# Layer 0 attention by four heads and 32 queries at a time, and score matmuls over 64 rows instead of 128

## The chip, the cores and the metric

The kernel runs on one core of one Trainium2 chip. The metric is the device time of one execution in microseconds (us). The engines of a core are TensorE (PE in the profile, with its weight loads as PEld), VectorE (DVE), ScalarE (ACT), GpSimd (POOL) and SyncE (SP), which here issues nearly all the DMAs. TensorE's clock has two levels, 1.2 and 2.4 GHz; the profile gives the granted clock as a share of the higher one.

## The reference

Fourteen sublayers run one after another on an input of 4 batches x 512 tokens x 128 features. Those that matter here are the attentions, all with 16 heads of 8 features:

```
x = x + _L0_attn_ref(_layernorm(x), ...)      # layer 0: a learned bias by distance q - k; keys further back
                                              # than the table of 32 distances get no weight
_L1_ffn_ref:  softmax attention over all earlier keys (causal), then gated experts     # twice
_L1_attn_ref: scores * beta, lower triangle, no softmax
_L2_attn_ref: softmax attention inside blocks of 32 tokens
_L3_attn_ref: softmax attention over all 512 keys
```

Layer 0's scores are `q k^T / sqrt(8) + bias[q - k]`. What the kernel keeps of the bias table is 32 rows (REL = 32), so a query looks at no more than the 31 keys before it and itself.

## The kernel before

**Slots.** The work is cut into 56 units (14 sublayers x 4 batches), and each unit into three parts: pre (normalize, project to q, k and v, bring q and k into the layout for the scores), core (the attention or expert work itself) and post (output projection, residual). The program is a row of 58 slots. In slot k the core of unit k, the pre of unit k+1 and the post of unit k-1 run beside each other, and a barrier of all engines ends the slot. Within a slot each engine has one fixed row of instructions. A table (SLOT_ORDERS, ORDERS) says in which order the three streams take turns on an engine: in "a3b1a1b4" a is the core, b the pre and c the post, and the number says how many steps. An engine waits at a semaphore in that row, and all behind it waits too.

**q and k for the scores.** q and k are split into three bf16 parts each, stacked to 64 columns per head (stack_parts), and turned by TensorE with two heads side by side, so that 128 rows hold two heads (turn_stacks: 8 pairs of heads through one bank of PSUM). k is copied as it stands (KX). q is copied twice per pair by copy_q, the upper half to one slot of QX and the lower half to another, where the other 64 rows are zeros. So score_rows gives 128 rows for q and for k, and the rows of the other head count for nothing. In the two rotary attentions (layers 2 and 3) clear_q writes those zeros first, since QX held other data.

**The scores in attend8** (l1_ffn, l2_attn, l3_attn): a first pass of score matmuls finds each row's maximum (L969, then for the causal kind a 128-row matmul that adds the mask, L972; DVE reduces at L1051); a second pass gives the scores transposed (L1000, mask L1003), ACT takes the exponential (L1094), and TensorE weighs v with it (L1017, 128 rows by 32 columns for each of four heads). Between them the maxima are put into q, which is turned and copied again (take_q, through copy_q, L427).

**Layer 0's core, attend_near.** 64 units: 16 heads x 4 blocks of 128 queries, each against the 256 keys (128 in the first block) up to its end. Per unit: a score matmul (L1139), an add of the bias with the row minimum (DVE L1194), the exponential with its sum (ACT L1173), reciprocal and scaling (DVE L1199, L1202), one or two turns (PE L1148), a copy (ACT L1181), and the weighing of v (PE L1160). The bias comes sheared out of DRAM: the pre writes q times the bias table there (L1257), and the core reads it back with a stride of one less than the row, one DMA per head (L1127), 16 in a core.

Of the kernel before, what the change touches and what calls it, by code (L numbers as in the profile page):

```python
# [30 lines left out]
P = 128  # L31
# [12 lines left out]
REL = 32  # L44
# [14 lines left out]
    [("ip_T", NI), ("pv", 4 * DV), ("l0_qkv", 3 * D), ("l0_out", 4 * D),  # L59
# [8 lines left out]
L0_COLS = NI + 4 * DV + 3 * D + 4 * D  # L68
# [146 lines left out]
def bank(m, i, n=512):  # L215
    return m.ps[:, i, 0:n]
# [198 lines left out]
def q_slot(h):  # L415
    return 4 * (h // 4) + 2 * (h % 2) + (h // 2) % 2


def score_rows(a, h):

    return a.QX[:, q_slot(h), :], a.KX[:, h // 2, :]


def copy_q(copy, a, pair, src):

    for e in range(2):
        ins = copy(a.QX[64 * e:64 * e + 64, q_slot(2 * pair + e), :], src[64 * e:64 * e + 64, :])  # L427
    return ins
# [6 lines left out]
def clear_q(nc, m, lane, a):  # L435

    cleared = lane.note("cleared")

    def gpsimd(pool):
        yield 0.0  # L440
        nc.gpsimd.memset(a.whole[:, 0:4096], 0.0).then_inc(cleared, 1)

    lane.add(0.1, gpsimd=gpsimd)
    return cleared, 1


def turn_stacks(nc, m, lane, a, stkk, ready, cleared=None):
# [15 lines left out]
    def take(eng, copy, pair):  # L463
        if cleared is not None and pair < 2:
            eng.wait_ge(*cleared)
# [444 lines left out]
def attend8(nc, m, note, a, kind):  # L910
# [194 lines left out]
def attend_near(nc, m, note, a, heads, rows_of, value_of, place_of, sheared):  # L1105
    units = [(h, qt) for h in range(heads) for qt in range(NT)]
    U = len(units)
    NS, NPR, NTB, NTS, NAV, NREL = 2, 6, 2, 4, 2, 3
    AVB = NS + NTB
    TURN, WEIGH = 3, 5  # L1110

    def width(qt):
        return 2 * P if qt else P

    scores, negmax, exps, inverted, scaled, turned, pT_ready, av, o_out = (note(n) for n in (
        "scores", "negmax", "exps", "inverted", "scaled", "turned", "pT_ready", "av", "o_out"))
    rel_in = [note(f"rel{i}") for i in range(NREL)]
    prob = m.core[:, 0:NPR * 2 * P].rearrange("p (a b) -> p a b", b=2 * P)
    pT = m.core[:, NPR * 2 * P:(NPR + NTS) * 2 * P].rearrange("p (a b) -> p a b", b=2 * P)
    rel = m.core[:, (NPR + NTS) * 2 * P:(NPR + NTS) * 2 * P + NREL * 2 * L].rearrange("p (h q j) -> p h q j", h=NREL, q=NT)  # L1120

    def sync(sp):
        for h in range(heads):
            yield max(0.0, NT * (h - NREL + 1) + 0.5)
            if h >= NREL:
                sp.wait_ge(negmax, NT * (h - NREL + 1))
            sp.dma_start(rel[:, h % NREL], sheared(h)).then_inc(rel_in[h % NREL], 16)  # L1127

    def tensor(pe):
        for i in range(U + WEIGH):  # L1130
            yield i
            if i < U:
                h, qt = units[i]
                nk = width(qt)
                k0 = (qt + 1) * P - nk
                q, k = rows_of(h)
                if i >= NS:
                    pe.wait_ge(negmax, i - NS + 1)
                nc.tensor.matmul(bank(m, i % NS, nk), q[:, qt * P:(qt + 1) * P], k[:, k0:k0 + nk],  # L1139
                                 start=True, stop=True).then_inc(scores, 1)  # L1140
            if TURN <= i < U + TURN:
                u = i - TURN
                nk = width(units[u][1])
                pe.wait_ge(scaled, u + 1)
                if u >= NTB:
                    pe.wait_ge(pT_ready, u - NTB + 1)
                for c in range(nk // P):
                    ins = nc.tensor.transpose(m.ps[:, NS + u % NTB, c * P:(c + 1) * P],  # L1148
                                              prob[:, u % NPR, c * P:(c + 1) * P], m.weight["ident"])
                ins.then_inc(turned, 1)  # L1150
            if i >= WEIGH:
                u = i - WEIGH
                h, qt = units[u]
                nc_ = width(qt) // P
                at, chunk, last = place_of(h)
                pe.wait_ge(pT_ready, u + 1)
                if at.start == 0 and qt == 0 and chunk >= NAV:
                    pe.wait_ge(o_out, chunk - NAV + 1)
                for c in range(nc_):
                    ins = nc.tensor.matmul(m.ps[at, AVB + chunk % NAV, qt * P:(qt + 1) * P],  # L1160
                                           value_of(h, qt + 1 - nc_ + c), pT[:, u % NTS, c * P:(c + 1) * P],
                                           start=(c == 0), stop=(c == nc_ - 1))
                ins.then_inc(av, 1)

    def scalar(act):
        for i in range(U + TURN):
            yield i + 0.6
            if i < U:
                nk = width(units[i][1])
                act.wait_ge(negmax, i + 1)  # L1170
                if i >= NPR:
                    act.wait_ge(turned, i - NPR + 1)
                nc.scalar.activation(prob[:, i % NPR, 0:nk], prob[:, i % NPR, 0:nk], ACT.Exp, bias=m.nm[:, i:i + 1],  # L1173
                                     scale=-1.0, accum_out=m.sums[:, i:i + 1]).then_inc(exps, 1)
            if i >= TURN:
                u = i - TURN
                nk = width(units[u][1])
                act.wait_ge(turned, u + 1)
                if u >= NTS:
                    act.wait_ge(av, u - NTS + 1)  # L1180
                nc.scalar.copy(pT[:, u % NTS, 0:nk], bank(m, NS + u % NTB, nk)).then_inc(pT_ready, 1)  # L1181

    def vector(dve):
        for i in range(U + WEIGH + 1):
            yield i + 0.3
            if i < U:
                h, qt = units[i]
                nk = width(qt)
                dve.wait_ge(scores, i + 1)
                if qt == 0:  # L1190
                    dve.wait_ge(rel_in[h % NREL], 16 * (h // NREL + 1))
                if i >= NPR:
                    dve.wait_ge(turned, i - NPR + 1)
                nc.vector.tensor_tensor_reduce(prob[:, i % NPR, 0:nk], bank(m, i % NS, nk),  # L1194
                                               rel[:, h % NREL, qt, 2 * P - nk:2 * P], 1.0, -NEG * 4,
                                               ALU.add, ALU.min, m.nm[:, i:i + 1]).then_inc(negmax, 1)
            if 1 <= i <= U:
                dve.wait_ge(exps, i)
                nc.vector.reciprocal(m.rsum[:, i - 1:i], m.sums[:, i - 1:i]).then_inc(inverted, 1)  # L1199
                dve.wait_ge(inverted, i)  # L1200
                p = prob[:, (i - 1) % NPR, 0:width(units[i - 1][1])]
                nc.vector.tensor_scalar(p, p, m.rsum[:, i - 1:i], None, ALU.mult).then_inc(scaled, 1)  # L1202
            if i >= WEIGH:
                u = i - WEIGH
                if u < U:
                    h, qt = units[u]
                    at, chunk, last = place_of(h)
                    if last and qt == NT - 1:
                        dve.wait_ge(av, u + 1)
                        nc.vector.tensor_copy(a.otok[:, chunk, :], bank(m, AVB + chunk % NAV)).then_inc(o_out, 1)  # L1210

    return [(U + WEIGH + 1.0, dict(tensor=tensor, scalar=scalar, vector=vector, sync=sync))]


# [3 lines left out]
def l0_attn_pre(nc, m, lane, a, b, l):  # L1218
# [6 lines left out]
    turn_stacks(nc, m, lane, a, s.stkk, stacked)  # L1225
    f = lane.fills(4)
    stored = lane.note("stored")
    shear = m.shear[a.p]

    def tensor(pe):  # L1230
        for r in range(4):
            yield 3.0 * r
            pe.wait_ge(lane.taken, f + r)
            for i in range(4):
                for qt in range(NT):
                    h = 2 * (4 * (r % 2) + i) + r // 2
# [1506 lines left out]
```

## Time and profile before

| | |
|---|---|
| Runs | 3664.6, 3666.59, 3658.38 us (median 3664.6) |
| The profiled execution | 3654.07 us, its span 3652.2 us |
| Granted TensorE clock, mean | 0.882 |
| PE, PEld, DVE, ACT, POOL busy | 81%, 51%, 66%, 53%, 25% of the span |
| Instructions | 63921, of them 23249 matmuls |
| Layer 0 attention cores | the four slots from 217.8 to 607.1 us |
| Causal cores (l1_ffn, twice) | the eight slots from 775.6 to 1111.6 and from 1375.6 to 1688.6 us |
| Layer 2 and layer 3 attention cores | four slots each, from 1924.0 and from 2794.0 us |

How to read it: the shares are means over slots with different limits. PE's busy time counts the latency of each matmul too, so that its share is not its load; the times from one matmul's start to the next one's tell more. A row of a group of instructions gives its line, engine, operation, output and inputs, for a matmul the tile of the array in use (rows*columns), the shape and the count, then busy time in us and the mean of one in ns, then the idle time before it and what ended it. The page's chain of waits covers only the last slot (its shares are 1% and less), and says nothing of the rest.

### The profile page before, as it was taken

What the parts mean: (1) busy time and instruction counts of PE and PEld (TensorE: products, weight loads), DVE (VectorE), ACT (ScalarE), POOL (GpSimd) and SP (SyncE); (2) the same over time, 40 slices, a digit from 0 to 9 for tenths busy, and PEclk for the clock granted to TensorE, in tenths of its full rate; (3) what the DMA queues carried; (4) which work ended last, traced back from release to release, by engine and by line L of the source; (5) the groups of instructions that cost most, each with busy time, mean ns of one, the idle gap of its engine ahead of it and who ended that gap; (6) DMA issues with size and microseconds to landing.
All of it is one profiled execution on the core that took longest, in us unless ns stands there. A gap on an engine that the chain in (4) does not pass through costs nothing. (4 is left out here: it accounts for less than half of the span.)

```text
span 3652.2 us, 63921 instructions
## 1 busy us (share of the span) xinstructions
PE 2966.9 (81%) x23249; PEld 1869.6 (51%) x23249; DVE 2404.7 (66%) x6402; ACT 1929.6 (53%) x5094; POOL 899.9 (25%) x875
## 2 busy tenths in 40 slices
PE   5868888878987558899787787889887889889875
PEld 3545544544443434456675587656554333556553
DVE  4667765677777456786456543868776677777752
ACT  2356775245553225555246633656664677667652
POOL 1000000011133331111213211635451112444430
PEclk7879988689988779999898988989998899999987
DMA  3423432000000000003660056300000000001010
GB/s 121 166 76 100 110 102 67 1 1 1 1 1 1 1 1 1 1 1 103 222 210 6 12 194 212 100 20 23 14 23 4 1 1 1 21 14 24 13 29 9
DMA packets 132658, 183.41 MB, mean 50 GB/s; under 512 B 48501, under 2 KB 108021, under 8 KB 130682
## 3 DMA queue, kind: packets, MB, share of 16 engines
q1 hardware_dynamic: 129818, 174.14, 15.3%
q8 instruction: 186, 3.05, 0.4%
q0 software_dynamic: 2048, 4.20, 0.3%
q14 instruction: 126, 1.03, 0.1%
q10 hardware_dynamic: 480, 0.98, 0.1%
HBM read 131.90 MB, written 30.61 MB: 44 GB/s over the span
## 5 line engine op out<-in xcount | busy, mean ns | idle before, releaser
L1051 DVE TENSOR_REDUCE nm<-ps 128x1 f32<-128x512 f32 (+4 forms) x832 | 443.3, 564 | 111.8 <-PE ps L972 63.7
L1094 ACT ACTIVATE core<-ps 128x512 f32<-128x512 f32 (+3 forms) x832 | 377.0, 510 | 131.0 <-PE ps L1003 91.7
L274 POOL TENSOR_TENSOR rstd<-ve,weights 128x4 f32<-128x4 f32 x80 | 80.9, 1011 | 1290.4 <-DVE ve L251 1289.9
L969 PE MATMUL ps<-hand 128*128 128x128 bf16 (+3 forms) x1024 | 302.4, 335 | 57.5 <-DVE nm L1051 31.2
L427 ACT COPY hand<-ps 64x512 bf16<-64x512 bf16 x448 | 259.6, 580 | 139.4 <-PE ps L459 100.7
L1000 PE MATMUL ps<-hand 128*128 128x512 bf16 (+3 forms) x1024 | 273.5, 309 | 18.6 <-ACT hand L427 9.4
L1890 POOL TENSOR_TENSOR pre<-pre,sin 128x512 f32<-128x512 f32 x128 | 221.9, 1754 | 241.3 <-ACT pre L1859 225.5
L2006 ACT ACTIVATE core<-ps,nm 128x128 f32<-128x128 f32 x512 | 181.8, 374 | 124.4 <-DVE nm L2021 123.7
L1659 PE MATMUL ps<-hand 128*128 128x128 f32 x1408 | 199.7, 302 | 38.5 <-DMA hand<-in_experts 38.5
L1895 POOL TENSOR_TENSOR ss<-ss,weights 128x16 f32<-128x16 f32 x64 | 194.2, 3035 | 117.4 <-DVE ss L1910 115.9
L1818 PE MATMUL ps<-weights,pre 128*128 128x512 f32 x384 | 207.1, 637 | 17.4 <-ACT pre L1862 17.3
L1659 PEld LDWEIGHTS ps<-hand 128*128 128x128 f32 x1408 | 187.6, 214 | 49.8 <-DMA hand<-in_experts 45.3
L1675 ACT ACTIVATE core<-ps,hand 128x128 f32<-128x128 f32 x352 | 100.7, 370 | 202.6 <-PE ps L1659 202.3
L969 PEld LDWEIGHTS ps<-hand 128*128 128x128 bf16 x1024 | 99.9, 104 | 198.1 <-DVE nm L1051 135.2
L459 PE MATMUL ps<-identb,hand 128*128 128x128 bf16 x768 | 83.8, 238 | 142.2 <-DVE pre L387 65.7
L1017 PE MATMUL ps<-core,hand 128*32 128x512 f32 (+3 forms) x2048 | 185.0, 451 | 8.7 <-ACT core L1094 5.3
L1000 PEld LDWEIGHTS ps<-hand 128*128 128x128 bf16 x1024 | 94.8, 99 | 185.3 <-ACT core L1094 102.8
L1689 DVE SCALAR_TENSOR_TENSOR core<-ps,hand,core 128x128 f32<-128x128 f32 x352 | 99.0, 344 | 133.2 <-ACT core L1675 132.0
L1173 ACT ACTIVATE core<-core,nm 128x256 f32<-128x256 f32 (+1 forms) x256 | 123.7, 483 | 107.8 <-DVE nm L1194 105.1
L1061 POOL CAST hand<-nm 128x16 bf16<-128x16 f32 x192 | 61.4, 320 | 463.9 <-DVE nm L1051 455.6
L427 DVE COPY hand<-ps 64x512 bf16<-64x512 bf16 x192 | 80.8, 421 | 137.4 <-PE ps L459 135.8
L1160 PE MATMUL ps<-core,hand 128*32 128x128 f32 x896 | 154.4, 294 | 0.0
(331 smaller groups left out, 7542.6 us busy)
## 6 DMA issues: line engine op xcount, KB each, us to landing
hand<-in_experts SPq DMA_DIRECT2D x88, 836.0 KB, 4.9
core<-shear SPq DMA_DIRECT2D x64, 512.0 KB, 3.8
shear<-post SPq DMA_DIRECT2D x64, 256.0 KB
hand<-hand SPq DMA_DIRECT2D x16, 512.0 KB, 4.4
hand<-hand SPq DMA_DIRECT2D x16, 384.0 KB, 5.6
pre<-sorted_in SPq DMA_DIRECT2D x8, 704.0 KB, 4.7
sorted_out<-core SPq DMA_DIRECT2D x88, 64.0 KB, 2.3
core<-in_stream SPq DMA_DIRECT2D x2, 2048.0 KB, 7.8
```

Of the source, the lines that this page charges most:

```text
L427: ins = copy(a.QX[64 * e:64 * e + 64, q_slot(2 * pair + e), :], src[64 * e:64 * e + 64, :])
L969: ins = nc.tensor.matmul(b[:, n * P:n * P + nk], q[:, qt * P:(qt + 1) * P], k[:, lo:lo + nk], start=kind != BLOCK32, stop=True, skip_group ...
L1000: ins = nc.tensor.matmul(b[:, n * P:n * P + z - s], k[:, kt * P:(kt + 1) * P], q[:, s:z], start=kind != BLOCK32, stop=True, skip_group_che ...
L1017: ins = nc.tensor.matmul(m.ps[32 * j:32 * j + 32, OUT, s:z], a.V[:, kt, 9 * h:9 * h + 32], prob8[:, (4 * f + j) % PROBS, n * P:n * P + z - s],
L1051: nc.vector.tensor_reduce(nm_of(h, qts), src, AX.X, ALU.max, negate=True).then_inc(negmax, 1)
L1094: nc.scalar.activation(prob8[:, i % PROBS, 0:L - q0], m.ps[:, RING[at % NR], 0:L - q0], ACT.Exp).then_inc(ring_out, 1)
L1160: ins = nc.tensor.matmul(m.ps[at, AVB + chunk % NAV, qt * P:(qt + 1) * P], value_of(h, qt + 1 - nc_ + c), pT[:, u % NTS, c * P:(c + 1) * P ...
L1659: ins = nc.tensor.matmul(m.ps[:, 2 * (i % 2) + s, c * P:(c + 1) * P], w1(i, s, c), a.xs[:, i * P:(i + 1) * P], start=True, stop=True)
L1818: nc.tensor.matmul(banks[at % N], s.hT[:, t * P:(t + 1) * P], qkv[:, l, i, :], start=True, stop=True).then_inc(lane.filled, 1)
L1890: ins = nc.gpsimd.tensor_tensor(o[:, :, :, z:z + hl], x[:, :, :, y0:y0 + hl], sn[:, t, :, z:z + hl].unsqueeze(2).to_broadcast([P, 2, LH, h ...
L1895: nc.gpsimd.tensor_tensor(m.ss[:, 1, 0:2 * LH], m.ss[:, 0, 0:2 * LH], m.weight["half"][:, 0:2 * LH], ALU.pow).then_inc(rooted, 1)
L2006: nc.scalar.activation(prob[:, i % NP3, r * P:(r + 1) * P], bank(m, S[i % 2])[:, r * P:(r + 1) * P], ACT.Exp, bias=m.nm[:, 4 * i + r:4 * i ...
```

## The change

1. Layer 0's core is written anew (attend_near goes, the code stands in l0_attn_core). 8 units: 4 groups of four heads x 2 halves of 256 queries. A unit's bank holds 8 blocks of 32 queries x 64 keys for four heads, the heads on 32 partitions each. 32 score matmuls of 64 rows by 32 columns make it, DVE adds the bias, takes minima and subtracts them (three instructions over 512 columns), ACT takes one exponential, four turns, one copy, and 32 small matmuls weigh v. The bias is read by 64 DMAs of 32 KB (16 per group), and each of the 32 descriptors x 4 is 256 bytes long.
2. The sums come from v's column of ones, so the post divides and then projects (divide, out_project), where it only projected before.
3. A second copy of v, shifted by 32 tokens (Vs), is made by two DMAs in the pre, after turn_stacks.
4. q is kept once: turned q and k of a pair are one copy of 1024 columns (QK), score_rows gives 64 rows, and copy_q, q_slot and clear_q go. All score matmuls of l1_ffn, l1_attn, l2_attn and l3_attn then use 64 rows; their masks are still 128-row matmuls.
5. The tables of orders are new for the slots with attentions.

```
@@ score_rows, turn_stacks
-    return a.QX[:, q_slot(h), :], a.KX[:, h // 2, :]
+    rows = slice(64 * (h % 2), 64 * (h % 2) + 64)
+    return a.QX[rows, h // 2, :], a.KX[rows, h // 2, :]
...
-        copy_q(copy, a, pair, lane.atb[:, 0:L])
-        copy(a.KX[:, pair, :], lane.atb[:, L:2 * L]).then_inc(lane.taken, 1)
+        copy(a.QK[:, pair, :], lane.atb).then_inc(lane.taken, 1)
@@ attend8, take_q
-            copy_q(nc.scalar.copy, a, 2 * g + n, m.psb[:, RING[at % NR], 0:L]).then_inc(ring_out, 1)
+            nc.scalar.copy(a.QX[:, 2 * g + n, :], m.psb[:, RING[at % NR], 0:L]).then_inc(ring_out, 1)
@@ l0_attn_pre
+    def vector(dve):
+        yield 0.0
+        dve.wait_ge(*stacks_turned)
+        nc.vector.memset(a.Vs[0:32, 0, :], 0.0).then_inc(none_set, 1)
     def sync(sp):
+        yield 0.1
+        sp.wait_ge(*stacks_turned)
+        sp.dma_start(a.Vs[32:128, :, :], a.V[0:96, :, :]).then_inc(moved, 16)
+        sp.dma_start(a.Vs[0:32, 1:NT, :], a.V[96:128, 0:NT - 1, :]).then_inc(moved, 16)
@@ l0_attn_core
+    units = [(g, half) for g in range(4) for half in range(2)]
+    BQ, BK = 32, 64
+    NPR, NTS, NREL = 3, 3, 2
+    def sync(sp):
+        for g in range(4):
+            yield max(0.0, 2.0 * (g - NREL + 1) + 0.6)
+            if g >= NREL:
+                sp.wait_ge(added, 2 * (g - NREL + 1))
+            for j in range(4):
+                for odd in range(2):
+                    for r in range(2):
...
+                        sp.dma_start(dst[:, :, odd, r], src).then_inc(rel_in[g % NREL], 16)
+        def score(i):
+            if half == 0:
+                nc.tensor.matmul(out[:, 0:BK], m.identb, m.far, start=True, stop=True)
+            for n, at, _, _ in blocks(half):
+                for j in range(4):
+                    q, k = score_rows(a, 4 * g + j)
...
+                    ins = nc.tensor.matmul(out[BQ * j:BQ * (j + 1), at:at + BK], q[:, BQ * n:BQ * (n + 1)], keys, ...)
+        def weigh(u):
+            for n, at, v, row in blocks(half):
+                for j in range(4):
+                    ins = nc.tensor.matmul(m.ps[BQ * j:BQ * (j + 1), O[row // BK], to:to + BQ],
+                                           v[row:row + BK, 9 * h:9 * h + 32], pT[row:row + BK, u % NTS, col:col + BQ], ...)
+    def vector(dve):
+            if half == 0:
+                dve.wait_ge(rel_in[g % NREL], 16 * 16 * (g // NREL + 1))
+            nc.vector.tensor_tensor(p, bank(m, S[i % 2]), rel[:, g % NREL, half * L:(half + 1) * L], ALU.add)
+            nc.vector.tensor_reduce(lows(i), eight(p), AX.X, ALU.min)
+            nc.vector.tensor_tensor(eight(p), eight(p), lows(i).unsqueeze(2).to_broadcast([P, 8, BK]), ALU.subtract)
@@ l0_attn_post
-    project_turned(nc, m, lane, a.otok, m.weight["l0_out"], m.x[b])
+    divided = divide(nc, m, lane, a.otok, m.post.ot)
+    out_project(nc, m, lane, m.post.ot, m.post.oT, m.weight["l0_out"], None, m.x[b], m.x[b], divided)
@@ the order of slots 5 and 6 (a core, b pre, c post)
-     "sync": "a15b1a1b4"},
+     "sync": "a3b1a1b5"},
```

On SP in a slot that holds layer 0's core of batch 1 and its pre of batch 2 (slot 5; slot 6 is the same). "core" is the bias buffer, "hand" the buffers that pre hands to core, "shear" the sheared bias in DRAM. Before:

```order
45 L1127 DMA core<-shear 128x4x256 x15
46 L1257 DMA shear<-pre 128x16x32
47 L1127 DMA core<-shear 128x4x256
48 L1257 DMA shear<-pre 128x16x32 x3
```

And of the change:

```order
46 L1183 DMA core<-shear 32x4x64 x48
47 L1122 DMA hand<-hand 96x672
48 L1123 DMA hand<-hand 32x504
49 L1183 DMA core<-shear 32x4x64 x16
50 L1132 DMA shear<-pre 128x16x32 x4
```

The fourth group's 16 bias loads stand behind the two moves of v, which wait for the end of turn_stacks.

On DVE in slot 6 of the change, from its start. L1246, L1249 and L1252 are the add, minimum and subtract of a unit; L371 begins stack_parts of the pre:

```order
436 L1246 TENSOR_TENSOR core<-ps,core 128x512
437 L1249 TENSOR_REDUCE nm<-core 128x8
...
443 L1246 TENSOR_TENSOR core<-ps,core 128x512
444 L1249 TENSOR_REDUCE nm<-core 128x8
...
448 L1246 TENSOR_TENSOR core<-ps,core 128x512
449 L1249 TENSOR_REDUCE nm<-core 128x8
450 L371 CAST hand<-pre 128x64x8
```

Two whole units, and the add and the minimum of the third (the first that needs the second group's bias), stand ahead of the pre's stacking.

On ACT in slot 7 (layer 0's core of batch 3 beside l0_ffn's pre, whose GELU is L727), of the change; L1260 is the core's exponential, L1267 and L1274 its copies:

```order
230 L727 ACT_TABLE_LOAD
231 L727 ACTIVATE pre,acc_pre<-ps 128x512
232 L1260 ACT_TABLE_LOAD
233 L1260 ACTIVATE core<-core 128x512
234 L1267 COPY core<-ps 128x512
235 L727 ACT_TABLE_LOAD
```

There are 14 loads of a table in this slot of the change, and 16 before.

## Rows read from the trace of the kernel before

**Rows 1.** Windows, last two layer 0 slots and sum: stretch, length, busy, PEclk, DMA share, GB/s.

```profile
406.50:493.90 87.40, 74.09 (x572) 46.65 (x572) 66.83 (x296) 61.45 (x224) 5.07 (x9) 0.94 0.41 109
493.90:607.10 113.20, 89.39 (x532) 51.48 (x532) 64.99 (x298) 77.21 (x227) 1.01 (x1) 0.83 0.26 75
sum 389.30, PE 318.69 PEld 195.06 DVE 272.76 ACT 264.52 POOL 16.28; mean PE 79.67 PEld 48.77 DVE 68.19 ACT 66.13 POOL 4.07
```

**Rows 2.** Groups of instructions in slot 6, 406.5 to 493.8 us.

```profile
L1173 ACT ACTIVATE core<-core,nm 128x128 f32<-128x128 f32 (+1 forms) x64 | 31.0, 484 | 24.2 <-DVE nm L1194 23.5
L1194 DVE CUSTOM_DVE_ANT_0 core<-ps,core 128x128 f32<-128x128 f32 (+1 forms) x64 | 24.8, 388 | 9.0 <-PE ps L1139 8.3
```

**Rows 3.** SP's timeline: start us, length us, then engine, line, operation, count.

```profile
84.11 21.42 SPq L2475 DMA_DIRECT2D shear<-post  x32
```

**Rows 4.** The bias loads of line 1127 by themselves, over the whole run.

```profile
L1127 SPq DMA_DIRECT2D core<-shear x64: 359/360/2142, 217.9 to 577.7; - x64
...
DMA to landing us min/median/max: 3.5/3.8/6.2
```

**Rows 5.** Groups by form, VectorE, whole run.

```profile
L2029 DVE TENSOR_TENSOR core<-core,rsum 128x512 f32<-128x512 f32 x128 | 97.1, 759 | 4.4
L2021 DVE TENSOR_REDUCE nm<-ps 128x4 f32<-128x512 f32 x128 | 87.8, 686 | 78.7 <-PE ps L1973 70.6 <-DMA post<-y 7.4
...
L468 DVE COPY hand<-ps 128x512 bf16<-128x512 bf16 x96 | 40.8, 425 | 1.3
```

**Rows 6.** Groups by form, ScalarE, whole run.

```profile
L427 ACT COPY hand<-ps 64x512 bf16<-64x512 bf16 x448 | 259.6, 580 | 139.4 <-PE ps L459 100.7 <-PE ps L983 32.6
...
L468 ACT COPY hand<-ps 128x512 bf16<-128x512 bf16 x96 | 56.3, 586 | 1.1
```

**Rows 7.** VectorE's timeline at the end of slot 17 (l1_attn), slot 18 begins in the last row.

```profile
1250.10 0.86 DVE L427 COPY hand<-ps 64x512 bf16<-64x512 bf16 x2 [4.02 <-PE ps L459]
...
1255.42 0.85 DVE L427 COPY hand<-ps 64x512 bf16<-64x512 bf16 x2 [4.02 <-PE ps L459]
...
1259.51 0.68 DVE L242 BATCH_NORM_STATS2 st<-x 128x6 f32<-128x128 f32 x3 [2.79 <-PEq L206]
```

**Rows 8.** ScalarE's table loads in slot 7.

```profile
L752 ACT ACT_TABLE_LOAD x8 | 10.3, 1283 | 0.1
L1173 ACT ACT_TABLE_LOAD x8 | 10.3, 1283 | 0.1
```

**Rows 9.** The first of the three instructions of a rank comparison, whole run.

```profile
L691 DVE TENSOR_SCALAR pre<-pre,acc_pre 128x128 bf16<-128x128 f32 (+3 forms) x64 | 33.0, 515 | 37.9 <-ACT pre L755 28.2 <-PE ps L704 9.3
```

**Rows 10.** Windows: one causal slot (slot 13), and the sum of all eight.

```profile
849.60:934.70 85.10, 77.37 (x584) 39.31 (x584) 66.45 (x188) 48.22 (x116) 14.12 (x31) 0.90 0.00 1
...
sum 649.00, PE 577.36 PEld 301.83 DVE 488.21 ACT 382.56 POOL 125.65; mean PE 72.17 PEld 37.73 DVE 61.03 ACT 47.82 POOL 15.71
```

**Rows 11.** TensorE's timeline in slot 13, matmuls alone.

```profile
871.25 0.23 PE L212 MATMUL ps<-rowparts,onesb 3*128 3x128 bf16 x1
871.41 0.39 PE L1000 MATMUL ps<-hand 128*128 128x512 bf16 x1
871.63 0.22 PE L1003 MATMUL ps<-identb,negcausal 128*128 128x128 bf16 x1
871.69 0.22 PE L969 MATMUL ps<-hand 128*128 128x128 bf16 x1
```

**Rows 12.** TensorE's timeline in slot 37 (layer 3's local attention).

```profile
2414.52 0.38 PE L1967 MATMUL ps<-negwin,identb 128*128 128x512 bf16 x1
2414.83 1.09 PE L1973 MATMUL ps<-hand 64*64 64x128 f32 x16
```

**Rows 13.** TensorE's timeline in slot 3.

```profile
208.85 0.17 PE L704 MATMUL ps<-onesb,post 128*128 128x1 bf16 x1
208.95 0.37 PE L814 MATMUL ps<-aggv,hand 64*128 64x1 f32 x1
```

**Rows 14.** Waits in slot 13: waiter, waited for, us in total, times, longest.

```profile
PEld ps L969 <- DVE nm L1051: 8.3, 18, 1.1
```

More of the change, by code:

```diff
@@ L412, in stack_parts, with turn_stacks @@
     return stacked, 3
-def q_slot(h):
-    return 4 * (h // 4) + 2 * (h % 2) + (h // 2) % 2
 def score_rows(a, h):
-    return a.QX[:, q_slot(h), :], a.KX[:, h // 2, :]
[L424 to L428, printed above, removed]
+    rows = slice(64 * (h % 2), 64 * (h % 2) + 64)
+    return a.QX[rows, h // 2, :], a.KX[rows, h // 2, :]
 def pair_of(stk, t, pair):
     return stk[:, t, 2 * pair:2 * pair + 2, :].rearrange("p a b -> p (a b)")
[L435 to L447, printed above, removed]
+def turn_stacks(nc, m, lane, a, stkk, ready):
     f = lane.fills(8)
@@ L1102, in attend8 @@
     return [(LEAD + total + 1.0, dict(tensor=tensor, vector=vector, gpsimd=gpsimd, scalar=scalar))]
[L1105 to L1212, printed above, removed]
@@ new lines, in l0_attn_core @@
+    U = len(units)
+    BQ, BK = 32, 64
+    NPR, NTS, NREL = 3, 3, 2
+    TURN, WEIGH = 2, 3
+    S, PT, O = (0, 1), (2, 3), (4, 5)
+    scores, added, least, shifted, exps, turned, pT_ready, av, o_out = (note(n) for n in (
+        "scores", "added", "least", "shifted", "exps", "turned", "pT_ready", "av", "o_out"))
+    rel_in = [note(f"rel{i}") for i in range(NREL)]
+    prob = m.core[:, 0:NPR * L].rearrange("p (s n) -> p s n", s=NPR)
+    pT = m.core[:, NPR * L:(NPR + NTS) * L].rearrange("p (s n) -> p s n", s=NTS)
@@ new lines, in scalar @@
+    def scalar(act):
+        for i in range(U + WEIGH + 1):
+            if i < U:
+                yield i + 1.4
+                act.wait_ge(shifted, i + 1)
+                nc.scalar.activation(prob[:, i % NPR, :], prob[:, i % NPR, :], ACT.Exp, scale=-1.0).then_inc(exps, 1)
+            if TURN <= i < U + TURN:
+                yield i + 1.6
+                u = i - TURN
+                act.wait_ge(turned, u + 1)
+                if u >= NTS:
+                    act.wait_ge(av, u - NTS + 1)
+                nc.scalar.copy(pT[:, u % NTS, :], bank(m, PT[u % 2])).then_inc(pT_ready, 1)
+            if i >= WEIGH and (i - WEIGH) < U and units[i - WEIGH][1] == 1:
+                yield i + 1.8
+                g = units[i - WEIGH][0]
+                act.wait_ge(av, i - WEIGH + 1)
+                own = a.otok[:, g, :].rearrange("p (t r n) -> p r t n", r=2, n=BK)
+                out = m.ps[:, O[0]:O[1] + 1, 0:L // 2].rearrange("p r (t n) -> p r t n", n=BK)
+                nc.scalar.copy(own, out).then_inc(o_out, 1)
@@ L2312, in macaron @@
             a.whole = whole
-            a.QX, a.KX = (whole[:, s:z].bitcast(BF16).rearrange("p (h n) -> p h n", n=L) for s, z in ((0, 4096), (4096, 6144)))
+            a.QK = whole[:, 0:4096].bitcast(BF16).rearrange("p (c n) -> p c n", c=8)
+            a.QX, a.KX = a.QK[:, :, 0:L], a.QK[:, :, L:2 * L]
             v = 6144
@@ L2400, in macaron @@
         m.EX = sb("EX", REL, dt=BF16)
+        m.far = sb("far", 64, dt=BF16)
         totals = [offsets(fields)[1] for fields in LEVELS]
```

279 lines of the change are left out of this document (172 added, 107 removed).

## Prediction

> **What bounds the kernel now.** The page's shares are means over 58 slots, and its chain of waits shows only the last slot, so I read the windows first, one per slot, then the groups inside a slot, and last the starts of single matmuls. Layer 0's four core slots take 389.3 us together, slot 6 87.4 and slot 7 113.2 [rows 1]. There no engine is full, but three are near it: of the 1.37 us that slot 6 has per unit (64 of them) PE is busy in 1.16, DVE in 1.04 and ACT in 0.96, and they hand the same tile round. ACT alone has 64 exponentials of 0.48 and stands 23.5 us before them, waiting for DVE's 64 adds [rows 2]. Slot 7 adds 16 table loads of 1.28 us [rows 8]. The eight causal slots take 649 us, PE busy in 577 of them [rows 10]. In these PE is packed: a mask starts 0.22 us after a 512-column score matmul and the next score 0.06 us after the mask [rows 11], which is one column per 0.42 ns with nothing between. So TensorE's own time is the bound in the second pass. Ahead of it, some 22 score matmuls wait for DVE's maxima, 8.3 us in all [rows 14].
>
> **Layer 0, slots 4 to 7.** The 64 units go, and with them nearly all of what rows 1 show as busy beside the pre. What comes is 8 units. On DVE each costs three instructions over 512 columns: 0.69 + 0.69 + 0.76 = 2.1 us [rows 5] (the add taken like the reduction), 17 us in all. On ACT 8 x 0.6 + 12 copies x 0.6 = 12 us [rows 6] (a copy of as many columns). On PE 64 small matmuls and 4 turns per unit. No row has a tile of 64*32; 16 matmuls on tiles of 64*64 take 1.09 us with 128 columns [rows 12], 0.07 each, so 64 lie between 64 x 0.025 and 64 x 0.07 = 1.6 to 4.5 us, and I take 2.5. The core by itself would then need 8 x 2.5 + 6 = 26 us.
>
> It won't get that, since SP must issue 64 bias loads where there were 16. The issue itself is 0.36 us long [rows 4]; 32 loads of 128 descriptors in a row took 21.42 us, 0.67 each [rows 3]. The new ones have 128 descriptors as well, so I take 0.65 and keep 0.36 as the other end. From issue to landing it is 3.8 us [rows 4]. A group of 16 then lands every 10.4 us: 14, 25, 35 and 45 us after the slot's start.
>
> - Slots 5 and 6: DVE's row has the add and minimum of the third unit ahead of the pre's stacking, so stacking starts at 26 rather than near 18. It takes 6 us. turn_stacks has 8 pairs. Now two pairs take 5.32 us [rows 7]. The copies of a pair shrink from 2 x 0.58 + 0.59 to about 1.0 on ACT and from 2 x 0.42 + 0.42 to about 0.8 on DVE (one copy of 1024 columns, from the fixed part and the slope between 0.58 for 64x512 and the time of 512 columns; an estimate from [rows 5, 6]), 0.6 us per pair and 4.9 per pre. That gives 8 x 1.9 = 15, and the stacks are turned at 47. Behind that on SP stand the two moves of v (1.3) and the last 16 loads (10.4), landed at 62.5. Two units on DVE (4.4) and the tail through exponential, turns, copy, weighing and the copy out (3.8), and the barrier (1): 71. At 0.36 per issue it is 58.
> - Slot 7: the last group lands at 45, DVE has all core steps ahead of the eight rank comparisons of the next l0_ffn. 45 + 4.4 + 8 x 1.3 (the first of three instructions is 0.5 [rows 9]) + 1.5 = 62; 14 table loads stay (18 us on ACT), which are hidden beside these loads. At 0.36: 50.
> - Slot 4: SP has all four groups ahead of the pre's stores, and the post of l0_ffn adds 10 us of DVE: 62, or 52.
>
> Sum 71 + 71 + 62 + 62 = 266, less about 4 for an issue between the two ends: 262 against 389, **-127 us**; the ends are 218 and 285. The longer post (16 turns, four reciprocals and products, one projection, about 8 us in a row) lies beside slots of over 60 us, in slot 8 beside the core of l0_ffn; I give it nothing, 2 us if it shows.
>
> **The causal slots.** The instructions are the same in number and columns, but 128 score matmuls per slot now use a tile of 64*128 with a 128*128 mask behind each. A change of tile has a price in this trace. K = 3 rows to 128: 0.16 us from start to start where 128 columns alone take 0.06 [rows 11], so 0.10. 128*128 to 64*64: 0.31 after 512 columns where 0.22 is due, so 0.09 [rows 12]. 128*128 to 64*128, the very pair: 0.10 after one column [rows 13]; before it such matmuls start every 0.025, so 0.07. I take 0.093. Along the order a slot has 79 changes before and 307 after, 228 more, 21 us. In the first 22 scores (44 changes, 4 us) PE waits for DVE anyway [rows 14]; of the rest some 3 us fall into other waits. That leaves 14 us per slot, for eight slots **+112 us**. The ends: 8 us each if the waits swallow twice as much (+64), 20 each if none (+160).
>
> The Trainium skill, TensorEngine Tiling (Array Packing), Key Properties, says that a change of tiling mode drains TensorE. It gives no figure; by that rule both ways cost, as I have counted.
>
> **Other slots.** Layer 3's full attention has no mask, so only 40 changes more per slot (+3.7), but successive heads now lie in different rows. In rows 12, 16 matmuls of 0.107 us of columns take 1.09 instead of 1.7 us: two tiles run at once. At 42 such neighbours of 0.2 us a slot could save 8. With four ACT us less in take_q I put -4 per slot, **-16** (from -30 to +12, if they don't overlap).
>
> The Trainium skill, TensorE: Matmul & The Clock Gate, Part 3, says that matmuls in different row groups run side by side. By that rule the whole 8 us per slot come where PE is the bound, by the rows on 64*64 tiles alone nothing is certain for 64*128.
>
> Layer 2: 62 changes more (5.8) against 4.9 less in turn_stacks and the 3.5 us clearing of q gone: 0. l1_attn: in slots 17 and 18 turn_stacks ends the slot [rows 7], -5 each; elsewhere it ends it with another stream beside it, -1 to -2 in five slots; 15 more changes in four slots hide behind GpSimd's powers. Together **-16** (-30 to +5).
>
> **Sum.** 3652.2 - 127 + 112 - 16 - 16 = 3605 us of span, 1.9 more for the execution. The profiled execution was 10.5 us under the median of the runs; the same step of -47 from 3664.6 gives **3617 us**.
>
> **Rivals.**
> A. The drains cost more than layer 0 saves. Place: the second pass of the causal slots. With +20 per slot, layer 3's overlap absent (+12), and layer 0 held at 285 by SP: 3664.6 + 160 + 12 - 104 - 10 = 3722. It decides from 13 us per causal slot at that layer 0, and from 20 at the layer 0 of my forecast. For it: PE is packed there [rows 11]. Against: the first pass waits for DVE.
> B. The drains hide. If a 64*128 and a 128*128 matmul follow each other without a gap, the causal slots gain 2 us each by the shorter copies, layer 3's slots 3.7 more than forecast, and all is 3664.6 - 127 - 16 - 31 - 16 = 3475. Against it are rows 11 to 13, all three with a gap.
> C. SP issues as fast as its instruction is long, 0.36 us: layer 0 falls to 218, and the time is 3573. For it: 0.36 in rows 4; against: rows 3.
> D. The change doesn't shorten layer 0 since the small tiles issue slowly: at 0.1 us per matmul a unit needs 6.4 us of PE, a core 51 us more or less as SP's loads allow; it would add 10 us per slot, 3657, no change. Little speaks for it.
>
> **Numbers.** Forecast as it stands 0.48, C or between 0.19, B 0.08, A 0.15, D 0.10. About 0.2%, 7 us, is what can be told from no change. Faster: forecast, C and B with a part of D, 0.79; within 0.2% 0.07; slower 0.14 (A, and the upper edge of the others). The likeliest's own range is 3575 to 3660. B and the far end of A are left out: 3540 to 3690.
>
> **What would show it.** Slots 4 to 7 near 62, 71, 71 and 62 us, SP's bias loads 0.65 apart, DVE's adds of units 0, 2, 4 and 6 waiting for the landing, in slots 5 and 6 the last of them after the moves of v. In the causal slots about 98 us instead of 85, and from a score's start to its mask's start 0.09 more than the columns. Layer 3's slots a few us shorter, with scores of two heads starting within 0.01 us. Wrong it is if causal slots stay at 85 (B), or if layer 0's last groups land before 30 us (C).

## The result and the profile after

The changed kernel takes 3902 us (median of four, 3881 to 3920) where the kernel before takes 3662: ratio 1.065, 95% interval 1.060 to 1.071. Forecast were 3617 us and a range of 3540 to 3690. It is slower by 240 us, on the side of rival A but far beyond it. The two profiled executions, from which the times of slots come, are 227 us apart.

The windows, cut at the slots, give first the last two core slots of layer 0 with the sum of all four (columns as in [rows 1]), then two causal slots with the sum of all eight, to be held against [rows 10].

```profile
342.03:409.13 67.10, 39.01 (x972) 29.25 (x972) 31.10 (x61) 22.31 (x45) 6.58 (x9) 0.63 0.34 54
409.13:464.97 55.84, 40.11 (x932) 27.13 (x932) 30.07 (x70) 36.90 (x54) 1.01 (x1) 0.68 0.26 40
sum 252.49, PE 158.71 PEld 115.72 DVE 130.07 ACT 105.68 POOL 20.76; mean PE 39.68 PEld 28.93 DVE 32.52 ACT 26.42 POOL 5.19
```

```profile
748.68:878.54 129.86, 127.41 (x584) 51.93 (x584) 66.54 (x180) 43.06 (x100) 12.91 (x31) 0.63 0.00 1
...
1769.51:1911.64 142.13, 140.00 (x543) 55.78 (x543) 61.99 (x183) 36.94 (x84) 12.20 (x27) 0.52 0.03 8
sum 1028.56, PE 1008.07 PEld 410.97 DVE 491.83 ACT 344.58 POOL 118.45; mean PE 126.01 PEld 51.37 DVE 61.48 ACT 43.07 POOL 14.81
```

Layer 0 gave back 137 us (389 to 252). The causal slots took 380 (649 to 1029). PE has as many instructions there as before (584 in slot 13), is busy 98% of the time, and its granted clock is 0.52 to 0.65 where it was 0.89 to 0.96. Everything else together is about -15: slot 3 -6, l1_attn -13, l3_attn -5, l2_attn +4.5, the rest +4.6.

The first causal slot of the changed kernel in five windows shows how the clock goes.

```profile
632.30:638.00 5.70, 4.59 (x16) 1.59 (x16) 5.09 (x19) 0.00 (x0) 3.23 (x6) 0.66 0.01 4
638.00:643.00 5.00, 4.71 (x20) 2.82 (x20) 4.40 (x13) 1.17 (x2) 0.00 (x0) 0.50 0.00 0
643.00:650.00 7.00, 7.00 (x24) 3.10 (x23) 3.03 (x7) 1.51 (x5) 1.25 (x5) 0.50 0.01 2
650.00:735.00 85.00, 84.87 (x424) 32.66 (x423) 36.33 (x80) 33.08 (x77) 6.49 (x18) 0.53 0.00 1
735.00:748.70 13.70, 12.20 (x130) 6.98 (x126) 3.25 (x6) 8.28 (x19) 0.00 (x0) 1.00 0.00 1
```

The clock falls to 0.50 (1.2 GHz) in the first scores and stays near it for 85 us of attention. The profile calls PE wholly busy there. It is back at 1.00 (2.4 GHz) only in the last 14 us, in which turns and other products over all 128 rows (24 of turn_stacks, 16 of the post) stand among the last scores. Whether these bring it back isn't shown.

The fall at the head of a causal slot is not new. The kernel before has it too, here in slot 13 (from 849.6), and the clock is back after 10 us:

```profile
850.00:860.00 10.00, 8.14 (x37) 2.80 (x36) 9.13 (x30) 0.00 (x0) 1.25 (x3) 0.55 0.01 2
860.00:870.00 10.00, 8.79 (x67) 6.36 (x66) 7.68 (x22) 4.71 (x9) 3.12 (x8) 0.94 0.00 0
```

By the clock's own record in the two traces, no stretch at the lower level lasts longer than 10.2 us in the eight causal slots of before. In the changed kernel each of the eight has one of 61 to 137 us. So what the change did is to keep the clock from coming back, more than to make it fall.

TensorE's timeline shows a pair of units in slot 13, first at the higher level, then at the lower (start us, length us).

```profile
771.10 0.39 PE L975 MATMUL ps<-hand 64*128 64x512 bf16 x1
771.41 0.23 PE L978 MATMUL ps<-identb,negcausal 128*128 128x128 bf16 x1
771.58 0.39 PE L944 MATMUL ps<-hand 64*128 64x512 bf16 x1
771.89 0.23 PE L947 MATMUL ps<-negcausal,identb 128*128 128x128 bf16 x1
...
787.58 0.29 PE L978 MATMUL ps<-identb,negcausal 128*128 128x128 bf16 x1
787.80 0.61 PE L944 MATMUL ps<-hand 64*128 64x512 bf16 x1
788.34 0.29 PE L947 MATMUL ps<-negcausal,identb 128*128 128x128 bf16 x1
788.57 0.39 PE L975 MATMUL ps<-hand 64*128 64x256 bf16 x1
```

At the higher level a mask starts 0.32 us after its 512-column score, 0.22 in [rows 11]: 0.10 for the change, as forecast, and 0.10 more for the way back. At the lower level it is 0.54, of which 0.43 are columns: the change costs 0.11 there, hardly more, and the columns cost double.

With that each start-to-start time can be split. For the eight causal slots I count the columns at the granted clock (twice for f32, and once where two products run side by side), the changes of tile shape at 0.105 us each (the table has their number), and what is left of the slots' time as waiting. So each row adds up: 649 = 445 + 552 x 0.105 + 146.

| kernel | causal slots, us | clock in them | columns, us | changes | waiting, us |
|---|---|---|---|---|---|
| before | 649 | 0.89 to 0.96 | 445 | 552 | 146 |
| after | 1029 | 0.52 to 0.65 | 697 | 2400 | 80 |
| e1: 128 rows | 649 | 0.90 to 0.96 | 444 | 552 | 147 |
| e12: 128 rows, no masks | 633 | 0.85 to 0.93 | 403 | 552 | 172 |
| e11: 64 rows, no masks | 686 | 0.66 to 0.87 | 437 | 883 | 156 |
| e2: 64 rows, masks of 64 rows | 726 | 0.65 to 0.91 | 499 | 883 | 134 |
| e3: 128 rows, masks of 64 rows | 934 | 0.74 to 0.89 | 587 | 2472 | 87 |
| e10: 64 rows, masks together | 872 | 0.59 to 0.89 | 603 | 1728 | 88 |

From before to after: 1848 changes more at 0.105 are +194 us, waiting -66, the same columns at a lower clock +252. That is the 380. Only e2 and e11 have products side by side in these slots (neighbours on opposite halves of the rows that start within 0.03 us): 557 and 211 pairs, which hide 44 and 47 us of columns. Their columns at the granted clock would be 543 and 484 without it.

### The profile page after: what moved, and what is told of

Its sections match the earlier page's. It is cut to its first block and busy times, and to the rows that moved or that the text cites. A ratio compares the mean times of both kernels' runs of the same rounds, so it can differ in the third digit from the quotient of the medians.

```text
span 3879.1 us, 64317 instructions
## 1 busy us (share of the span) xinstructions
PE 3279.5 (85%) x24849; PEld 1889.7 (49%) x24849; DVE 2237.5 (58%) x5304; ACT 1653.9 (43%) x4088; POOL 865.9 (22%) x867
## 5 line engine op out<-in xcount | busy, mean ns | idle before, releaser
L1026 DVE TENSOR_REDUCE nm<-ps 128x1 f32<-128x512 f32 (+4 forms) x832 | 457.3, 564 | 436.4 <-PE ps L947 364.1
L1069 ACT ACTIVATE core<-ps 128x512 f32<-128x512 f32 (+3 forms) x832 | 397.8, 505 | 475.4 <-PE ps L978 409.3
L944 PE MATMUL ps<-hand 64*128 64x128 bf16 (+3 forms) x1024 | 344.6, 389 | 45.7 <-DVE nm L1026 25.6
L975 PE MATMUL ps<-hand 64*128 64x512 bf16 (+3 forms) x1024 | 304.1, 357 | 3.2 <-ACT core L1069 2.5
L992 PE MATMUL ps<-core,hand 128*32 128x512 f32 (+3 forms) x2048 | 230.4, 546 | 5.6 <-ACT core L1069 3.8
L975 PEld LDWEIGHTS ps<-hand 64*128 64x128 bf16 x1024 | 83.4, 97 | 257.2 <-issue 127.5
L944 PEld LDWEIGHTS ps<-hand 64*128 64x128 bf16 x1024 | 90.3, 101 | 192.5 <-DVE nm L1026 93.4
L443 ACT COPY hand<-ps 128x1024 bf16<-128x1024 bf16 x96 | 97.5, 1016 | 139.8 <-PE ps L437 139.5
L443 DVE COPY hand<-ps 128x1024 bf16<-128x1024 bf16 x96 | 66.3, 691 | 143.2 <-PE ps L437 143.0
L1978 PE MATMUL ps<-hand 64*64 64x128 f32 (+1 forms) x2048 | 146.8, 288 | 0.0
L947 PE MATMUL ps<-negcausal,identb 128*128 128x128 bf16 x512 | 143.4, 280 | 0.0
```

Of the source, the lines that this page charges most:

```text
L443: copy(a.QK[:, pair, :], lane.atb).then_inc(lane.taken, 1)
L944: ins = nc.tensor.matmul(b[:, n * P:n * P + nk], q[:, qt * P:(qt + 1) * P], k[:, lo:lo + nk], start=kind != BLOCK32, stop=True, skip_group ...
L975: ins = nc.tensor.matmul(b[:, n * P:n * P + z - s], k[:, kt * P:(kt + 1) * P], q[:, s:z], start=kind != BLOCK32, stop=True, skip_group_che ...
L992: ins = nc.tensor.matmul(m.ps[32 * j:32 * j + 32, OUT, s:z], a.V[:, kt, 9 * h:9 * h + 32], prob8[:, (4 * f + j) % PROBS, n * P:n * P + z - s],
L1026: nc.vector.tensor_reduce(nm_of(h, qts), src, AX.X, ALU.max, negate=True).then_inc(negmax, 1)
L1069: nc.scalar.activation(prob8[:, i % PROBS, 0:L - q0], m.ps[:, RING[at % NR], 0:L - q0], ACT.Exp).then_inc(ring_out, 1)
```

## The experiments

Times of slots are from each kernel's profiled execution, whole times are medians (of two runs for e2, e3, e8, e10, e11 and e12, of four or five for the others), and each ratio is to the kernel before timed beside it (3653 to 3669 us). The edits are shown shortened.

**e1_l0_part.** The layer 0 half alone:

```diff
-            q, k = score_rows(a, h)
+            q, k = all_rows(a, h)   # a.QX[:, q_slot(h), :], a.KX[:, h // 2, :], as before
```

> The layer 0 half of the change alone: the new core, its Vs moves, its divide post; q is kept in zero-filled slots again and every attention but layer 0's reads 128 rows. If the two halves only add, the slots 4 to 7 come to the 252 us of the changed kernel (389 before) and the eight causal slots to the 649 us of before, at a granted clock of 0.89 to 0.96: 3662 - 137 = about 3525 us. If the loss of the causal slots came in part from layer 0 or from the rest of the change, these slots stay over 700 us and the kernel over 3580.

3529 us, ratio 0.965 (0.962 to 0.969). The causal slots are those of before to 0.1 us:

```profile
725.27:810.39 85.12, 77.42 (x584) 39.32 (x584) 66.41 (x188) 48.18 (x116) 14.12 (x31) 0.90 0.00 1
...
sum 648.88, PE 576.02 PEld 301.34 DVE 488.08 ACT 382.30 POOL 125.64; mean PE 72.00 PEld 37.67 DVE 61.01 ACT 47.79 POOL 15.71
```

So layer 0's half costs the causal slots nothing. Layer 0's slots are 267, not 252: the shorter copies of the q half are worth 14 us there.

**e8_q_once.** The other half alone, on the layer 0 of before (with attend_near, whose scores then come by way of the 64-row score_rows).

```diff
-    return a.QX[:, q_slot(h), :], a.KX[:, h // 2, :]
+    rows = slice(64 * (h % 2), 64 * (h % 2) + 64)
+    return a.QX[rows, h // 2, :], a.KX[rows, h // 2, :]
```

> The q half of the change alone, on the layer 0 of before. If the halves add: 3902 + 3653 - 3529 = about 4026 us, with the eight causal slots near the 1029 us of the changed kernel. Layer 0's core then scores over 64 rows too and changes tile shape 3 times a unit instead of twice, so up to 4080 if that costs clock in slots 4 to 7 as it does in the causal slots. Under 3980 would mean that the new layer 0 itself worsened what follows.

4099 us, ratio 1.118 (1.113 to 1.123), beside a before of 3669. The causal slots take 1056 and layer 0's 442, 53 more than before. That is beyond the sum of the halves: the old layer 0 core scores over 64 rows there too, and the causal slots are 27 us longer than in the changed kernel with the same code, 20 of them in slot 14 (149 us for 130, at a clock of 0.50 for 0.63). What made that slot slower isn't shown. The loss is all in this half.

**e2_masks64.** No change of shape inside a unit:

```diff
-                ins = nc.tensor.matmul(b[:, nk - P:nk], m.identb, m.negcausal, start=False, stop=True, ...)
+                rows = slice(64 * (h % 2), 64 * (h % 2) + 64)
+                for other in (0, 1):   # second copies of both with their halves swapped
+                    ins = nc.tensor.matmul(b[:, nk - P:nk], m.eyes[rows, other, :], m.causals[rows, other, :], ...)
```

> The changed kernel, with each causal mask product of 128 rows replaced by two of 64 rows on the head's own half, so that a score and its mask have one tile shape. It has one 128-column product more per score, and no tile-shape change inside a unit. Theory W (the waits at tile-shape changes pull the granted clock down): the clock in the causal slots comes back to 0.88 or more and their sum from 1029 to about 650 us, the kernel to about 3520. Theory R (products over 64 rows, half of the array's rows, do not hold the clock, with or without the waits): the clock stays at 0.50 to 0.68, only the waits themselves go (about 256 of 0.105 us a slot, less some 7 us for the added products), the sum falls to about 890 us and the kernel to about 3765.

3584 us, ratio 0.980 (0.976 to 0.984).

```profile
788.84:878.07 89.23, 82.56 (x712) 44.74 (x712) 66.15 (x180) 40.84 (x100) 14.03 (x31) 0.89 0.01 1
...
1492.15:1598.77 106.62, 101.40 (x671) 52.91 (x671) 60.07 (x183) 34.51 (x84) 12.21 (x27) 0.65 0.04 10
sum 726.15, PE 668.94 PEld 364.40 DVE 482.15 ACT 325.88 POOL 124.01; mean PE 83.62 PEld 45.55 DVE 60.27 ACT 40.74 POOL 15.50
```

With 128 products more in a full slot it is 302 us shorter in the causal slots: 1517 changes fewer are 159, the columns are 198 less (44 of them hidden side by side), and 54 come back as waiting. Most of the clock is back (0.89 in slot 14), not all (0.65 in slot 23). Theory R, that 64 rows alone hold the clock down, falls in its strong form. W, that only the waits do (650 us were expected by it), is not whole either.

**e3_drains128.** e1 with the same masks: 128-row scores, as many changes as in the changed kernel.

> e1_l0_part with the masks alone as two products of 64 rows: the scores fill 128 rows, and there are as many tile-shape changes as in the changed kernel. Theory W: the granted clock in the causal slots falls to about 0.6, their sum is near 1030 us and the kernel near 3900. Theory R: the clock stays at 0.85 or more, a slot gains 256 changes of 0.105 us less what idle hides, and some 5 us of added products: 25 to 30 us a slot, a sum of 850 to 890 us and the kernel near 3740.

3822 us, ratio 1.046 (1.040 to 1.051).

```profile
753.75:870.95 117.20, 113.90 (x712) 49.38 (x712) 68.10 (x188) 50.58 (x116) 14.11 (x31) 0.84 0.00 1
...
1601.27:1727.39 126.12, 122.95 (x712) 52.39 (x712) 68.27 (x188) 50.66 (x116) 14.10 (x31) 0.76 0.00 1
...
sum 934.00, PE 906.71 PEld 399.60 DVE 503.28 ACT 402.17 POOL 123.93; mean PE 113.34 PEld 49.95 DVE 62.91 ACT 50.27 POOL 15.49
```

285 us over e1: 1920 changes 202, 1024 added products of 0.055 us 56, waiting -60, and 87 from the clock, which falls to 0.74 to 0.89. That lies between the two theories (1030 and 850 to 890 us; the sum is 934). About as many changes went with 252 us of clock where the scores fill 64 rows too. The masks of e3 fill 64 rows as well, so this isn't changes alone.

**e11_64_no_mask, e12_128_no_mask.** The cleanest pair: the causal masks are left out of the changed kernel and of e1.

```diff
-            if kind == CAUSAL:
-                ins = nc.tensor.matmul(b[:, nk - P:nk], m.identb, m.negcausal, ...)
```

> The changed kernel with the causal mask products left out (its causal attentions then see all keys up to the block's end): 64-row scores with no tile-shape change between them and no product added. If 64-row products alone do not hold the clock, it stays at 0.75 or below in the causal slots and their sum above 750 us. If only the waits at the changes pulled it down, it is 0.9 as in e12_128_no_mask and the sum 600 to 640, the kernel about 3470 to 3500. If both count, each in part, the clock is 0.80 to 0.88 and the sum 640 to 700.

> e1_l0_part with the causal mask products left out too: 128-row scores, the partner of e11_64_no_mask. A mask product takes 0.055 us of TensorE, 128 of them 7 us a slot; part of that turns into waiting for DVE, so the causal slots fall from 649 to 600 to 625 us at a clock of 0.92 or more, and the kernel from 3529 to about 3490. If the masks' columns were what held the clock up, it falls below 0.88.

3541 and 3518 us (ratios 0.969, 0.966 to 0.972, and 0.963, 0.960 to 0.966). Slot 13 and the sum, first of e11, then of e12:

```profile
708.42:801.39 92.97, 86.38 (x456) 35.24 (x456) 64.34 (x180) 40.44 (x100) 13.87 (x31) 0.69 0.00 1
...
sum 685.67, PE 610.81 PEld 257.36 DVE 473.53 ACT 321.81 POOL 123.65; mean PE 76.35 PEld 32.17 DVE 59.19 ACT 40.23 POOL 15.46
```

```profile
722.22:800.88 78.66, 68.96 (x456) 31.45 (x456) 65.83 (x188) 47.99 (x116) 14.13 (x31) 0.93 0.00 1
...
sum 632.77, PE 543.89 PEld 247.96 DVE 485.11 ACT 380.29 POOL 125.48; mean PE 67.99 PEld 31.00 DVE 60.64 ACT 47.54 POOL 15.69
```

With the same products and columns, and no mask, 64 rows cost 53 us. By the split above that is 35 for 331 changes (those to the turns and the weighing), 34 for the columns, and 16 less waiting. The 34 is what remains of a larger loss: without the 47 us that run side by side in e11, the lower clock costs some 80. So with few changes 64 rows go with a lower clock too. The sum is what was expected if both count in part (640 to 700), the clock is lower than that (0.66 to 0.87 for 0.80 to 0.88). e11 even has a lower clock than e2, which has more products in each unit. My 600 to 625 for e12 was too low: of 56 us of masks left out only 16 came off, 25 turned into waiting, and the clock fell a little.

**e10_masks_together.** Fewer changes, nothing else:

```diff
-            shifted_score(i)      # score, mask
-            score(LEAD + i)       # score, mask
+            side_by_side(shifted_score(i), score(LEAD + i))   # score, score, mask, mask
```

> The changed kernel with another order inside a step of the causal attention: both scores over 64 rows first, then both masks over 128, so that 42 of the 64 steps change tile shape 2 times instead of 4: 84 of some 300 changes of a slot fewer. If a change only costs its own 0.093 to 0.105 us, the causal slots come from 1029 to about 960 us and the kernel to about 3830. If the waits at the changes also hold the clock down, their clock rises from 0.59 to 0.70 or more, and the sum falls below 900, the kernel below 3780.

3714 us, ratio 1.017 (1.014 to 1.019); the causal slots 872. Of the 157 us less, 672 changes are 71 by themselves and the clock is 94, while 8 come back as waiting. A good quarter of the changes gone gives back over a third of what the clock had cost.

**e4_l1_l3_64.** e1 with 64-row scores in l1_attn and l3_attn, and the long copies of q.

```diff
-                    q, k = all_rows(a, 4 * g + j)
+                    q, k = score_rows(a, 4 * g + j)   # a.QX[rows, q_slot(h), :]; likewise where kind is FULL
```

> e1_l0_part, but the scores of l1_attn and of l3_attn read 64 rows (q still in its zero-filled slots, so the copies are those of before). If the 13 us that slots 16 to 19 and the 5 us that slots 44 to 47 gained in the changed kernel come from scores of two heads running side by side, they are here again: 18 us below e1_l0_part, about 3507. If they come from the shorter copies of q instead, it equals e1_l0_part. If the 64 rows cost clock there too, l3_attn's clock is under 0.90 and the kernel no faster than e1_l0_part.

3553 us, ratio 0.972 (0.969 to 0.975), so slower than e1. l1_attn is 264.5 as in e1 (264.1). l3_attn's four slots are 366 where e1 has 346, at a clock of 0.81 to 0.88. The changed kernel's -13 and -5 thus came from shorter copies, and reading 64 rows cost layer 3 some 20 us, though 127 of its score neighbours start side by side.

**e5_pairs64.** e2, with the heads of a step on opposite halves:

```diff
-        return 4 * g + j, second[u]
+        return 4 * g + (j ^ SWAP), second[u]   # SWAP is 1 in the causal and the full attention
-            shifted_score(i)
-            score(LEAD + i)
+            side_by_side(shifted_score(i), score(LEAD + i))
```

> e2_masks64 (3584 us), with the shifted score and the score of one step taken from heads on opposite halves of the rows and issued one after the other (score, score, mask halves alternating), in the causal and in the full attention, so that the two run side by side. If overlap is worth what its columns are, the causal slots lose some 36,000 columns each at 2.4 GHz, part of it into stalls: about 5 us a slot, and layer 3's four slots about 5 each: 3584 - 60 = about 3525 us. If the granted clock goes by how many rows work at a time, the clock in the causal slots also comes up from the 0.65 to 0.91 of e2_masks64 to above 0.88 everywhere, and the time is 3480 to 3500. If instead more overlap means fewer busy cycles and a lower clock, the clock falls below that of e2_masks64 and the time is 3584 or more.

3535 us, ratio 0.964 (0.961 to 0.967). The causal slots are 684 (e2 726), layer 3's 333 (e2 344), with the clock at 0.76 to 0.93. In the causal slots that is the 40 us expected: 743 pairs start side by side where e2 has 557, the columns are 42 us less, and changes and waiting are the same. A part of the 42 is a slightly higher clock. In layer 3 it is half of the 20 expected. The overlap doesn't make 64 rows better than 128 in the causal slots (649).

**e6_two_layouts, e7_loads_first, e9_full_pairs.** Short copies and 64 rows in layer 0, l1_attn and l3_attn; zero-filled q and 128 rows in the causal and block attention, cleared by GpSimd before. e7 moves one thing in two slots, e9 adds the heads of e5 in the full attention:

```diff
-     "sync": "a3b1a1b5"},
+     "sync": "a4b6"},
...
+    SWAP = int(kind == FULL)
-        return 4 * g + j, second[u]
+        return 4 * g + (j ^ SWAP), second[u]
```

> The new layer 0; q kept once and read over 64 rows in layer 0, l1_attn and l3_attn; zero-filled q, 128 rows, cleared by GpSimd ahead of each use (3.5 us), in the causal and block attentions. From e1_l0_part (3529): slots 3 to 7 get the shorter copies of the changed kernel (-20 us), slots 16 to 19 its -13, slots 44 to 47 its -5: about 3491 us, if the clears lie beside other work. If a clear at the head of GpSimd's queue delays the norm of the same pre, slots 11 and 19 are 3 to 4 us longer: about 3498. If the losses of 64-row reads that e4_l1_l3_64 showed in layer 3 (+20) count here too, about 3511.

> e6_two_layouts with one thing moved: in slots 5 and 6 SyncE issues the 16 bias loads of the last group ahead of the two Vs moves (which wait 17 us for the stacks), not behind. If these loads are what ends the slots, as the prediction had it, each of the two is 7 to 10 us shorter: 14 to 20 us below e6_two_layouts. If the copies or TensorE end them, within 3 us of it.

> e7_loads_first, with the shifted score's head taken from the other half of the rows in the full attention alone, so that it runs beside the score that is issued next to it. In e5_pairs64 the four slots of layer 3 came to 333.5 us so, against 344 to 348 in e6 and e7: 10 to 14 us below e7_loads_first (3500), about 3488. If the gain there was luck of the clock, the slots stay near 345 and the time at 3500.

3508, 3500 and 3490 us; ratios 0.958 (0.955 to 0.960), 0.955 (0.952 to 0.958) and 0.956 (0.954 to 0.958). All three beat both kernels. Their times don't tell them apart; single slots do. e6 is 17 us above its forecast by the median (beside a before of 3669, where the forecast built on 3653), 4 by its profiled span (3495); slots 3 to 7 are 20 us shorter than in e1 and l1_attn 11, as expected, and layer 3 only 1. SyncE's timeline in slot 6, of the changed kernel and of e7:

```profile
342.09 25.19 SPq L1183 DMA_DIRECT2D core<-shear  x48
383.92 0.53 SPq L1122 DMA_DIRECT2D hand<-hand  x1
384.49 0.60 SPq L1123 DMA_DIRECT2D hand<-hand  x1
385.43 10.90 SPq L1183 DMA_DIRECT2D core<-shear  x16
396.38 5.20 SPq L1132 DMA_DIRECT2D shear<-pre  x4
```

```profile
335.09 38.25 SPq L1219 DMA_DIRECT2D core<-shear  x64
376.10 0.53 SPq L1158 DMA_DIRECT2D hand<-hand  x1
```

The queue stood 17 us for the stacks with 16 loads behind it. With these ahead, slots 5 and 6 take 60.6 and 60.9 us instead of 68.3 and 66.4 (7 to 10 us each were expected). In e9 the layer 3 slots are 338 (e7 348), and TensorE's timeline has the two scores of a step side by side, twice:

```profile
2859.70 0.39 PE L1009 MATMUL ps<-hand 64*128 64x512 bf16 x1
2859.71 0.39 PE L978 MATMUL ps<-hand 64*128 64x512 bf16 x1
...
2860.58 0.39 PE L1009 MATMUL ps<-hand 64*128 64x512 bf16 x1
2860.58 0.39 PE L978 MATMUL ps<-hand 64*128 64x512 bf16 x1
```

That this is worth 10 us is less sure than it looks. Seven kernels have the layer 3 code of e7, and their four slots range from 341 to 348 us, with e7 the slowest. Against them e9 (338) and e5 (333) are 3 to 14 us shorter.

## Why the prediction was wrong

**The failed step is the causal slots, forecast at +112 us, measured at +380.** The forecast left the columns at what they cost in [rows 10, 11], at a clock of 0.90 and up, and added only the changes. Its own two parts were near: 21 us of changes per slot less 7 of cover, and measured 24 less 8. What it left out is that the same columns ran at 0.52 to 0.65 of the clock, +252 us. Neither the sum nor a rival had a term for that. Without the 252 the kernel would be near 3650 by this sum, inside the range. The profile shows the granted clock slot by slot, at 0.83 in slot 7 [rows 1] and 0.90 in slot 13 [rows 10], and the prediction never asked whether the changed instructions would still hold it.

Why it stayed low is settled in part. Many changes with scores over all rows lower it (e3), half-filled scores with few changes lower it (e11 against e12), both together lower it most (after), and taking out changes step by step gives it back (e10, e2). No run has either alone: e3's masks fill half of the rows, and e11 has 331 changes more than e12 and pairs side by side. How the loss divides between the two, and what exactly the chip weighs, stays open. The Trainium skill, TensorE: Matmul & The Clock Gate, Part 1, says that the clock is set by how busy TensorE has lately been. If busy were the profile's busy share, the trace would speak against it: 84.87 of 85.00 us at 0.53.

**Layer 0** was right: -137 for -127, the slots 63.1, 66.4, 67.1 and 55.8 for 62, 71, 71 and 62. The terms inside were off and made up for each other. SP's loads started 0.47 apart in the median, not 0.65, and landed 2.0 us after their issue, not 3.8. The tail behind DVE's last subtraction was 7.1 to 7.5 us in slots 5 and 6, not 4.8. PE's clock is 0.63 over these slots, which may be why. In slots 5 and 6 it was the stacks and the moves of v ahead of the last group that held it, as forecast, and e7 shows it.

**Other slots.** Copies: two pairs are 3.96 us apart where they were 5.32 [rows 7], and slots 16 to 19 give -13 of the -16 forecast for all these slots:

```profile
1262.52 0.69 DVE L443 COPY hand<-ps 128x1024 bf16<-128x1024 bf16 x1 [3.27 <-PE ps L437]
1266.48 0.69 DVE L443 COPY hand<-ps 128x1024 bf16<-128x1024 bf16 x1 [3.27 <-PE ps L437]
```

Layer 3: -5 for -16. The two scores of a step lie in the same half of the rows and don't overlap (0.23 us from start to start). But the score of one step and the shifted score of the next lie on opposite halves, and these did start together, as the prediction's sign had it. L944 is the score, L975 the shifted one:

```profile
3234.78 0.39 PE L944 MATMUL ps<-hand 64*128 64x512 bf16 x1 [0.37 <-DVE nm L1026]
3234.78 0.39 PE L975 MATMUL ps<-hand 64*128 64x512 bf16 x1
3235.38 0.39 PE L944 MATMUL ps<-hand 64*128 64x512 bf16 x1 [0.21 <-DVE nm L1026]
3235.38 0.39 PE L975 MATMUL ps<-hand 64*128 64x512 bf16 x1
```

In the four slots 120 neighbours start so, 30 a slot where 42 were forecast, and they hide 25 us of columns at the higher level. The changes took 17 of that back (188 to 353), a lower clock (0.88 on average for 0.92) another part, and the waiting stayed (76 us, then 73): in the lines shown each step waits for DVE's maxima. So the overlap came and paid little.

l2_attn: +4.5 for 0, all of it in slot 31, +13.6 at a clock of 0.63 (before 0.84); the four slots take 189 to 203 us in the other kernels that read 64 rows there. The drains that rival B would have hidden are all there, and D's small tiles are fast: layer 0's scores on 64*32 start 5 ns apart in the median.

## What to carry to other kernels

When a change keeps TensorE's columns but alters how full its array is or how often it waits between them, price the clock first: columns cost double at the lower level, and here that was 252 us where the changes themselves were 194. Put masks in the tile shape of the scores they belong to, or keep the zero-filled operand where TensorE is the bound, and use short tiles where another engine is. Judge the halves of a combined change apart: one alone gave a ratio of 0.965 (0.962 to 0.969), the other 1.118 (1.113 to 1.123).

## What the runs showed of the hardware

- A change between 64*128 and 128*128 costs 0.103 and 0.106 us at the higher clock level, and 0.11 at the lower: it hardly scales with the clock, unlike columns.
- Two 64*128 products on opposite halves start 0.00 to 0.01 us apart (e9, and the changed kernel's layer 3), on the same half 0.23 for 512 columns (the median of 118 such neighbours in the changed kernel).
- The profile's busy share of PE counts waits at changes and says nothing of the clock: 98% busy at 0.52 to 0.65.
- SyncE issued layer 0's loads (128 pieces of 256 bytes) 0.474 us apart in the median, the stores of [rows 3] 0.67.
- The clock's stretches at the lower level last at most 10.2 us in the causal slots of the kernel before, and up to 137 us in the changed one, with PE busy 98% of the time there.
